# Delta attention on one core: large products issued in parts between small ones, and other places for clippings, additions and token factors

## The reference, cut

```python
def step(carry, inp):
    S, R = carry
    q_t, k_t, v_t, a_t, aR_t, b_t, g_t = inp
    kn = k_t / jnp.maximum(jnp.linalg.norm(k_t, axis=-1, keepdims=True), 1e-12)
    pred = jnp.einsum('bhji,bhj->bhi', S, kn)
    r = jnp.clip(v_t - pred, -CLIP, CLIP)
    S = a_t[..., None] * S
    kp = jnp.einsum('bhd,bhde->bhe', kn, S)
    S = S + b_t[..., None, None] * kn[..., None] * (v_t - kp)[..., None, :]
    o = jnp.einsum('bhji,bhj->bhi', S, q_t)
    R = aR_t[..., None] * R
    kpR = jnp.einsum('bhd,bhde->bhe', kn, R)
    R = R + g_t[..., None, None] * kn[..., None] * (r - kpR)[..., None, :]
    o = o + jnp.einsum('bhji,bhj->bhi', R, q_t)
    return ((S, R), o)
```

## Time and profile before

| what | value |
|---|---|
| median of 3 runs | 3724.8 us (3717.01 to 3728.99) |
| profiled execution | 3720.78 us, of which the span is 3719.0 us |
| TensorE busy | 3255.9 us, 88% of the span |
| VectorE busy | 2569.9 us, 69% |
| ScalarE busy | 1383.9 us, 37% |
| GpSimd busy | 951.1 us, 26% |
| DMA | 168.17 MB, mean 45 GB/s |
| steady periods of `chunked_delta` | 29 in 2129.30 us |

### The profile page before, as it was taken

The page is one execution under the profiler, slowest core; times in us unless marked ns, Lnnn a source line. Parts: engine busy times, 40 slices in busy tenths (PEclk is TensorE's granted clock), DMA queues, the critical chain, the costliest instruction groups (busy, mean ns, idle before and its releaser), DMA issues. The chain is left out here.

```text
span 3719.0 us, 141826 instructions
## 1 busy us (share of the span) xinstructions
PE 3255.9 (88%) x62854; PEld 2466.6 (66%) x62854; DVE 2569.9 (69%) x5676; ACT 1383.9 (37%) x3203; POOL 951.1 (26%) x1051
## 2 busy tenths in 40 slices
PE   7775999997799999998999999989999999848888
PEld 4564999996566666766676676666666766535555
DVE  6873111111788788878887887778878888828887
ACT  2221222222345444444444444445444444421111
POOL 2343222221222322232222223222322232211110
PEclk9886999998899999999999999999999999979998
DMA  2116666673000000000000000000000000010000
GB/s 68 53 49 223 182 187 188 185 250 90 8 8 7 12 8 8 10 10 8 7 10 9 8 7 10 9 8 7 11 9 8 8 12 6 5 46 16 23 23 13
DMA packets 98174, 168.17 MB, mean 45 GB/s; under 512 B 15400, under 2 KB 71976, under 8 KB 97312
## 3 DMA queue, kind: packets, MB, share of 16 engines
q1 hardware_dynamic: 76976, 136.07, 11.0%
q0 software_dynamic: 19440, 21.97, 4.2%
q10 hardware_dynamic: 1152, 1.06, 0.1%
HBM read 118.86 MB, written 38.09 MB: 42 GB/s over the span
## 5 line engine op out<-in xcount | busy, mean ns | idle before, releaser
L1066 POOL TENSOR_TENSOR da_M<-da_M,da_decay 128x512 f32<-128x512 f32 x256 | 269.4, 1075 | 732.5 <-DVE da_prev_end L1178 408.6
L1373 ACT COPY da_Ub<-da_U 32x256 f32<-32x256 f32 x1024 | 412.1, 402 | 17.1
L1203 DVE TENSOR_TENSOR da_eGn<-da_eGn,da_z 128x30 f32<-128x30 f32 (+14 forms) x960 | 352.1, 367 | 32.9
L1202 DVE TENSOR_TENSOR da_z<-da_eGn 128x30 f32<-128x30 f32 (+14 forms) x960 | 344.2, 359 | 27.6
L1668 PE MATMUL da_C<-da_Ub,da_Km 128*64 128x256 f32 x2048 | 298.9, 411 | 3.8 <-issue 1.6
L840 PEld LDWEIGHTS le_ps_qkv<-le_scr,le_up 128*128 128x128 f32 x2272 | 265.9, 193 | 4.8 <-ACT le_scr L670 1.8
L840 PE MATMUL le_ps_qkv<-le_scr,le_up 128*128 128x128 f32 x2272 | 267.9, 277 | 1.2 <-ACT le_scr L670 1.2
L1499 PE MATMUL da_unit<-early_buffer,da_xnT 128*128 128x512 f32 x512 | 259.2, 630 | 5.5 <-ACT da_xnT L1319 2.3
L1506 PE MATMUL da_unit<-da_xnT,early_buffer 128*128 128x128 f32 x2048 | 247.1, 277 | 9.9 <-ACT da_eGn L1358 9.9
L1506 PEld LDWEIGHTS da_unit<-da_xnT,early_buffer 128*128 128x128 f32 x2048 | 238.2, 192 | 19.0 <-ACT da_eGn L1358 17.4
L1226 DVE TENSOR_TENSOR da_M<-da_C,da_M 128x512 f32<-128x512 f32 x256 | 176.2, 688 | 72.5 <-PE da_C L1668 68.6
(11 more groups left out here) (299 smaller groups left out, 7057.1 us busy)
## 6 DMA issues: line engine op xcount, KB each, us to landing
le_up<-in_upT SPq DMA_DIRECT2D x71, 1024.0 KB, 5.1
le_scr<-moe_slots SPq DMA_DIRECT2D x71, 129.0 KB, 4.3
le_down<-in_downT SPq DMA_DIRECT2D x8, 1024.0 KB, 12.1
early_buffer<-in_x SPq DMA_DIRECT2D x16, 256.0 KB, 4.0
moe_acc<-le_y SPq DMA_DIRECT2D x32, 128.0 KB, 2.3
da_x<-moe_acc SPq DMA_DIRECT2D x128, 32.0 KB, 1.8
stream<-da_xz SPq DMA_DIRECT2D x128, 32.0 KB, 1.6
stream<-da_y POOLq DMA_DIRECT2D x128, 32.0 KB, 3.0
```

The source lines that it names most:

```text
L1066: ins = nc.gpsimd.tensor_tensor(st_, st_, decay[:, par, rec, 2 * g:2 * g + 2].rearrange("p a b -> p (a b)").unsqueeze(2).to_broadcast([P, ...
L1202: c.link(tt(t, Xm[:, s + 1:C, s:s + 1].to_broadcast([P, below, s]), Xm[:, s:s + 1, 0:s].to_broadcast([P, below, s]), ALU.mult))
L1203: c.link(tt(Xm[:, s + 1:C, 0:s], Xm[:, s + 1:C, 0:s], t, ALU.add))
L1373: ins = nc.scalar.copy(Ub[rows_of(b), :, :, b, :], U[rows_of(b), rec])
```

## The change

`rates` and `values` take one more argument, `kk`, and issue one of the two products of a call; `norms_of_keys` is issued in two halves and `result` in four parts of two pairs of heads. In TensorE's period these parts stand between runs of small products. `result` stood between `queries` 0 and `queries` 1 near the period's start, and now surrounds the last two grams, `state_predicted(2)` and `solve(2, 0)`. The two last grams stand ahead of `solve(2, 0)`, `state_outputs(2)` and `inner_predicted(2)`, and `state_update(1, 1)` ahead of `state_rows(2)`. On ScalarE `result` follows `solved(2, 0)`. On VectorE `products` (1, 1), (0, 0) and (1, 0) are issued earlier, and those of half 0 wait for a new semaphore `rows_read`, which TensorE's `state_outputs(1)` raises; `clipped(2)` moves from between the last two `gram_out` to behind `triangle_in`; the substitution is split at other tokens, with `state_rows(3)`, `add_bias` 2, `update` (2, 1), `clipped(3)` and `update(3, 0)` between its parts; `update(3, 1)` follows `triangle_out`. The banks of `unit` are dealt out anew, and the waits for them with it. GpSimd's and SyncE's lists are unchanged.

```diff
-        RATE_BANK = (0, 2, 1, 2)
+        RATE_BANK = (0, 2, 0, 0)
...
-        OUT_BANK = (2, 0, 0, 0)
-        BANKS, GRAMS = ((1, 2), (0, 1), (1, 2), (0, 1)), (2, 3, 0, 1)
+        OUT_BANK = (2, 2, 2, 0)
+        KEY_BANK = (1, 0, 2, 0)
+        BANKS, GRAMS = ((1, 2), (0, 1), (1, 2), (1, 2)), (2, 3, 0, 1)
...
                 need(dve, g_ready, n * 6 + ((2, 3), (6, 5))[rec][half])
                 need(dve, q_ready, n * 2 + 2)
                 need(dve, km_ready, (n - 1) * NG + 4)
+                if half == 0:
+                    need(dve, rows_read, n)
...
                     decays(pn, 1)
+                if state:
+                    state_rows(i, 2)
+                    update(i, 1, 1)
+                if prepare:
                     gram_out(n, pn, 0)
-                if state:
-                    clipped(i, par, 2)
-                if prepare:
                     gram_out(n, pn, 1)
                     triangle_in(n, pn)
                 if state:
+                    clipped(i, par, 2)
                     update(i, 2, 0)
                 if prepare:
                     substitute(1, 6)
+                if norm:
+                    add_bias(i + 2, 2)
+                if prepare:
+                    substitute(6, 7)
                 if state:
                     state_rows(i, 3)
+                if prepare:
+                    substitute(7, 9)
+                if state:
                     update(i, 2, 1)
-                if norm:
-                    add_bias(i + 2, 2)
-                if prepare:
-                    substitute(6, 11)
+                if prepare:
+                    substitute(9, 12)
                 if state:
                     clipped(i, par, 3)
                 if norm:
                     add_bias(i + 2, 3)
-                if prepare:
-                    substitute(11, 14)
                 if state:
                     update(i, 3, 0)
                 if prepare:
-                    substitute(14, 20)
+                    substitute(12, C - 1)
+                    triangle_out(n)
                 if state:
                     update(i, 3, 1)
-                if prepare:
-                    substitute(20, C - 1)
-                    triangle_out(n)
...
                     solved(i, 2, 0)
+                if put:
+                    result(i - 1)
+                if state:
                     turned_outputs(i, 0)
                     solved(i, 2, 1)
                     turned_outputs(i, 1)
...
-            def rates(n, par, u):
-                if u == 0:
+            def rates(n, par, u, kk):
+                if kk == 0 and u == 0:
                     need(pe, xT_ready, n + 1)
                     need(pe, g_ready, (n - 1) * 6 + 6)
-                elif u == 1:
+                elif kk == 0 and u == 1:
                     need(pe, gram_done, once(n - 1, 0))
-                elif u == 2:
-                    need(pe, gram_done, once(n - 1, 3))
-                else:
-                    need(pe, a_ready, n * 4 + 2)
-                    need(pe, km_ready, once(n - 1, 0))
+                elif kk == 0:
+                    need(pe, a_ready, n * 4 + (1, 3)[u - 2])
+                    need(pe, gram_done, once(n - 1, 1))
+                    need(pe, out_ready, n - 2)
                 bank, cols = un[:, RATE_BANK[u]], slice((u % 2) * 512, (u % 2 + 1) * 512)
-                for kk in range(KD):
-                    ins = mm(bank, xnT[:, par, kk, :], wx[:, kk, u // 2, cols], start=(kk == 0), stop=(kk == KD - 1))
-                ins.then_inc(a_psum, 1)
+                ins = mm(bank, xnT[:, par, kk, :], wx[:, kk, u // 2, cols], start=(kk == 0), stop=(kk == KD - 1))
+                if kk == KD - 1:
+                    ins.then_inc(a_psum, 1)
...
-            def result(i):
-                need(pe, oT_ready, (i + 1) * NG)
-                if exists(i + 1):
-                    need(pe, km_ready, once(i + 1, 3))
-                for hp in range(NHP):
+            def result(i, part):
+                if part == 0:
+                    need(pe, oT_ready, (i + 1) * NG)
+                    if exists(i + 2):
+                        need(pe, gram_done, once(i + 2, 1))
+                    elif exists(i + 1):
+                        need(pe, km_ready, once(i + 1, 3))
+                for hp in (2 * part, 2 * part + 1):
                     ins = mm(un[:, 0, 0:D], oT[:, hp, :], wo[:, hp, :], start=(hp == 0), stop=(hp == NHP - 1))
-                ins.then_inc(out_psum, 1)
+                if part == 3:
+                    ins.then_inc(out_psum, 1)
 
...
                     inner_outputs(i, par, 1, 1)
+                    state_update(i, 1, 1)
                     state_rows(i, par, 2)
-                    state_update(i, 1, 1)
+                if put:
+                    result(i - 1, 0)
+                if prepare:
+                    gram(n, pn, 0)
+                if put:
+                    result(i - 1, 1)
+                if state:
                     state_predicted(i, par, 2)
+                if prepare:
+                    gram(n, pn, 1)
+                if put:
+                    result(i - 1, 2)
+                if state:
                     solve(i, 2, 0)
                     state_outputs(i, par, 2)
-                if prepare:
-                    gram(n, pn, 0)
+                if put:
+                    result(i - 1, 3)
                 if state:
                     inner_predicted(i, par, 2)
-                if prepare:
-                    gram(n, pn, 1)
-                if state:
                     state_update(i, 2, 0)
...
```

More of the change, by code:

```diff
@@ L1252, in period @@
                 if prepare:
-                    products(n, pn, 1, 1)
+                    products(n, pn, 0, 0)
+                    gram_out(n, pn, 2)
+                if state:
+                    clipped(i, par, 1)
                 if norm:
@@ L1404, in period @@
                     queries(n, 0)
-                if put:
-                    result(i - 1)
-                if prepare:
                     queries(n, 1)
@@ L1537, in gates, with norms_of_keys @@
                 ins.then_inc(bg_psum, 1)
-            def norms_of_keys(n):
-                need(pe, q_ready, n * 2 + 1)
-                need(pe, k_ready, n * 2 + 2)
-                for hp in range(NHP):
+            def norms_of_keys(n, half):
+                if half == 0:
+                    need(pe, q_ready, n * 2 + 1)
+                    need(pe, k_ready, n * 2 + 2)
+                for hp in range(half * HB, (half + 1) * HB):
                     ins = mm(un[:, 1, 2 * hp:2 * hp + 2], sq[:, hp, :], sel[:], start=True, stop=True)
-                ins.then_inc(n_psum, 1)
+                if half == 1:
+                    ins.then_inc(n_psum, 1)
             def growth(n, rec, part):
@@ L1817, in _ @@
             for u in range(4):
-                rates(0, 0, u)
+                for kk in range(KD):
+                    rates(0, 0, u, kk)
             pe.wait_ge(loaded, 16 * LOADS)
@@ L1821, in _ @@
             turned_outputs(NCH - 1, 3)
-            result(NCH - 1)
+            for part in range(4):
+                result(NCH - 1, part)
 def fp4_feed_forward(nc, x_in, consts, w, x_out, T, I):
```

147 lines of the change are left out of this document (74 added, 73 removed).

## The result

The changed kernel takes 3841.6 us (median of 4 runs, 3827.5 to 3844.4), the kernel before 3720.9: a ratio of 1.032, 95% interval 1.028 to 1.036. It is 121 us slower; the forecast was no change, 3724 us, with 3785 as the upper end. The profiled execution took 3827.5 us, 106.7 us above that of before.

What follows compares the result with a forecast made beforehand. The bound was a serial loop of TensorE's stage one and VectorE-bound stage two, 73.4 us a period. Stage one 31.4 plus stage two 42.3 made 73.7 us, taken as no change: 3724 us, range 3650 to 3785.

Steps and rivals of the forecast that it cites:

- The bound and the two stages: Per chunk: stage one, TensorE's first solve to next fourth gram, 35.5 us; stage two, VectorE's triangle solve, 37.8 us, VectorE-bound.
- The cuts: Large TensorE products issued in parts between small ones: gain 3.4 to 4.4 us in stage one, taken as 3.9.
- The rival that the cuts give nothing: Blocks not the cause: stage one stays near 35.3 us, period 77.6 us, 3855 us; chance 0.04.
- the blocks: TensorE's program arrives in blocks of some 256 records; one that runs in under about 3.6 us waits for the next.
- the +0.4 for weights loaded anew: Stage one on TensorE: three more cuts reload weights behind small products, 0.1 to 0.2 us each, +0.4 us.
- The new wait: rows_read holds VectorE in stage one until state_outputs(1) has read the token factors; claimed cost: nothing.
- The clipping: clipped(2), four VectorE instructions, moves behind triangle_in into stage two: +1.75 us.
- The border moves: In stage one, solve(2,0), state_outputs(2), inner_predicted(2) go behind last gram, -2.0 us; two quarters of result ahead of it, +1.8.
- The rescalings: Four GpSimd rescalings behind the late put_out fall beside stage two's substitution and delay VectorE: +2.8 us, range 2.0 to 3.3.
- The one-step-for-each rule: In the substitution, each GpSimd rescaling delays one short VectorE step: 4.1 us for four steps needing at most 1.2.
- Free as long as TensorE is back at the next first solve in time: In stage two, TensorE's solve(3,0) and solve(3,1) wait for VectorE some 2.3 and 1.2 us, at no cost.
- The second rival: TensorE bounds stage two if its clock falls to 1.2 GHz behind a wait: period 75.2 us, 3781 us; chance 0.16.

Runs made afterwards that it cites:

- e7: The kernel before with the rescaling of group 2 moved to the next period, beside group 3: 3696.7 us.
- e1: The changed kernel with GpSimd issuing the rescalings of groups 0 and 1 ahead of put_out: 3735.7 us.
- e9: e8 with clipped(2) between the last gram evictions and solve(2,0), state_outputs(2), inner_predicted(2) ahead of the last gram again: 3727.7 us.
- e2: The kernel before with GpSimd's rescalings of groups 0 and 1 held until update(2,0), put_out staying early: 3808.9 us.
- e3: The changed kernel with the rescalings of groups 0 and 1 ahead of put_out but held until update(2,0): 3808.5 us.
- e5: e1 with three 128x256 products that nobody reads added on TensorE ahead of solve(0,0): 3666.0 us.
- e8: e1 with the edit of e7 as well, so that no rescaling lies beside the substitution: 3676.7 us.

## Why the prediction was wrong

**The bound and the two stages** were right: e7 took 1.25 us from VectorE's work and stage two followed by 1.20.

**The cuts** were right in kind. Stage one was to lose 3.4 to 4.4 us of gaps and clock and come to 31.4; at full clock it came to 30.2, and TensorE's idle time in it fell from 4.2 to 0.9 us. The clock gave nothing (0.95 before, 0.93 after). The rival that the cuts give nothing is out; the blocks as their reason fit and were not tested apart. Of the 4.1 us on issue, 0.4 lay in stage two and were not stage one's to lose, and the +0.4 for weights loaded anew had no row: both kernels have 62,854 weight loads, and at a clock of 1.00 TensorE is busy 29.2 us in stage one, 30.1 before.

**The new wait** `rows_read` costs VectorE 28.8 us in 30 periods, in stage one, where it idles 9.6 us on average anyway: nothing, as said. **The clipping**, with all else that moved within stage two, cost 1.9 us (39.7 of e1 less 37.8) for 1.75 predicted. **The border moves** gained, 1.3 us net (e9).

**The rescalings** were placed rightly and priced too low: 2.8 us, range 2.0 to 3.3, against 4.7. The one-step-for-each rule was read from two rescalings on an idle GpSimd. It holds for four as well when GpSimd waits first and starts behind the first instruction (2.9 and 3.1 in e2 and e3), but not right behind `put_out`, and the step that put them there stood in the same paragraph. It had them start some 7 us into stage two, behind the first instruction at 6.7; their record starts at 6.5. This mis-sized term is 1.9 us of the period's miss, the largest part.

**"Free as long as TensorE is back at the next first solve in time"** is the step that failed in kind. The wait of `solve(3,0)`, 3.2 to 4.4 us instead of the 2.3 worked out, is followed by 1.2 GHz in every period, and the wait for the triangle, which the prediction did not price at all, in 16 of 29. The second falls into stage one, where TensorE is the bound: low clock costs 2.0 us there, 0.9 before. Taking `result` out of the place where VectorE hid it was counted as nothing lost there; it had kept TensorE busy up to the solve. The second rival had the mechanism, with a chance of 0.16, but in stage two and with TensorE as the bound there. In fact VectorE covers the low clock there: it idles 3.1 us of the changed kernel's stage two and 3.0 of e1's, whose clock is 1.00.

By the steps: 73.7 predicted, + 1.9 (rescalings), + 0.9 (stage one 32.3 for 31.4: 1.2 better at full clock, 2.0 lost to the clock), + 0.2 (the clipping's 1.9 for 1.75, and rounding) make the 76.7 measured.

## What to carry to other kernels

An engine that waits at a stage's end because another bounds it is not idle for free if its clock may be lower when it goes on: leave the work there that fills the wait, or move work in. A late producer of one small result also moves everything queued behind its consumer in order; look up what those instructions will stand beside. And a cost read from two instructions that start after a wait is not yet the cost of four that stand right behind other work in the queue.

## What was not expected of the hardware

- Four GpSimd instructions queued right behind its DMA issues hold a 30-element VectorE instruction for 4.04 us, three of the four; started by a wait, just behind that instruction, each lets one through, about 1.0 us each. Whether the queue or the start makes the difference was not settled.
- Three products a period that nobody reads, 1.5 us of work, save 70 us of 3736 when they fill a wait of TensorE of 1.5 to 2.0 us.
- Waits of one length, 0.6 to 0.7 us in e5, are followed by 1.2 GHz in some periods and not in others; waits of 1.1 us are in 24 of 27 periods of e8 and in 2 of 13 of the changed kernel.
